# Maximum over the partitions on GpSimd in place of two small matmuls, with four adapter groups computed later

## The reference, cut to what matters

```python
# x (2, 2048, 512), cond (2, 128); norm_w (512, 128), up_w (4096, 512), down_w (512, 2048)
scale = cond @ norm_w.T + 1.0
ms = jnp.mean(x * x, axis=-1, keepdims=True)
h = x * (scale[:, None, :] * jax.lax.rsqrt(ms + EPS))
u = h @ up_w.T
val, gate = jnp.split(u, 2, axis=-1)
h = val * jax.nn.gelu(gate, approximate=False)
x = act_quant(h) @ weight_quant(down_w).T + x
# the second layer: an adapter whose weights depend on cond
Wd_b = Wd + ((cond @ Wdd.T + bdd) * 0.1).reshape(B, BN, D)      # Wdd (65536, 128)
Wu_b = Wu + ((cond @ Wdu.T + bdu) * 0.1).reshape(B, D, BN)
down = jax.nn.relu(jnp.einsum('bld,bnd->bln', x, Wd_b) + bd)
out = x + jnp.einsum('bln,bdn->bld', down, Wu_b) + bu
```

## Time and profile before

| | us |
|---|---|
| median of 3 runs (865.81 to 866.25) | 865.9 |
| the profiled execution | 866.98 |
| its span, first to last instruction | 865.2 |
| TensorE busy | 846.8 (98%) |
| VectorE busy | 608.4 (70%) |
| ScalarE busy | 389.9 (45%) |
| GpSimd busy | 73.9 (9%) |

### The profile page before, as it was taken

How to read it: one execution, slowest core, us unless ns; L and a number is a source line. 1 busy time by engine, 2 the same in 40 slices (tenths; PEclk the granted TensorE clock), 3 DMA queues, 4 the chain that set the end, 5 groups by cost and what they waited for, 6 DMA issues and landing times.

```text
span 865.2 us, 11930 instructions
## 1 busy us (share of the span) xinstructions
PE 846.8 (98%) x4026; PEld 373.9 (43%) x4026; DVE 608.4 (70%) x942; ACT 389.9 (45%) x632; POOL 73.9 (9%) x79
## 2 busy tenths in 40 slices
PE   6999999999999999999999999999999999999998
PEld 5334444444444444444444444444444444444443
DVE  5997666888897765547886664658986764445986
ACT  5678776767545542216545543216433332214000
POOL 0453223210200000000200000000200000000100
PEclk9999999999999999999999999999999999999999
DMA  9879988659788876556587674634447443432231
GB/s 347 308 242 306 332 282 306 219 174 325 246 297 303 312 252 219 204 192 206 207 309 240 230 277 144 203 108 137 144 133 223 137 160 119 159 104 85 98 122 73
DMA packets 64283, 183.50 MB, mean 212 GB/s; under 512 B 7008, under 2 KB 8032, under 8 KB 64224
## 3 DMA queue, kind: packets, MB, share of 16 engines
q1 hardware_dynamic: 63936, 182.48, 60.5%
q10 hardware_dynamic: 288, 0.26, 0.1%
HBM read 152.31 MB, written 29.36 MB: 210 GB/s over the span
## 4 chain that ended last, share of the span: by engine, by line
PE 90%; ACT 3%; DVE 3%; DMA 2%; issue 2%; SPq 0%; POOL 0%; ACTq 0%; DVEq 0%; POOLq 0%
PE aux_ps L1114 10%; PE b_ps L1025 9%; PE b_ps L1029 9%; PE b_ps L1027 9%; PE a_ps L1025 6%; PE a_ps L1027 6%; PE a_ps L1029 6%; PE aux_ps L1070 6%; PE aux_ps L1177 3%; PE aux_ps L1168 3%; PE c_ps L1029 3%; PE c_ps L1027 3%; PE c_ps L1025 3%; PE e_ps L1027 3%; PE e_ps L1029 3%; PE e_ps L1025 3%
## 5 line engine op out<-in xcount | busy, mean ns | idle before, releaser
L1513 DVE SCALAR_TENSOR_TENSOR h_ring<-v_sb,unscale,gelu 128x512 f32<-128x512 f32 x63 | 48.4, 768 | 97.7 <-ACT gelu L836 54.8
L812 ACT ACTIVATE b_ps<-a_ps 128x512 f32<-128x512 f32 x63 | 36.7, 582 | 152.7 <-PE a_ps L1029 152.7
L1025 PE MATMUL b_ps<-t_mov,u_l 128*128 128x512 f16 x252 | 95.5, 379 | 1.6 <-DVE c_ps L1474 1.6
L1029 PE MATMUL b_ps<-t_mov,u_l 128*128 128x512 f16 x252 | 95.5, 379 | 0.0
L1027 PE MATMUL b_ps<-t_mov,u_l 128*128 128x512 f16 x252 | 95.5, 379 | 0.0
L1537 DVE TENSOR_TENSOR hmax<-gelu,hmax 128x512 f32<-128x512 f32 x120 | 82.4, 687 | 6.6 <-ACT gelu L842 1.0
L1114 PE MATMUL aux_ps<-h_ring,wq 128*128 128x512 f16 x384 | 84.9, 379 | 0.3
L711 POOL PARTITION_ALL_REDUCE yscale<-hmax x8 | 17.9, 2266 | 603.0 <-DVE hmax L1537 602.3
L842 ACT ACTIVATE gelu<-h_ring 128x512 f32<-128x512 f32 x64 | 40.3, 630 | 53.0 <-DVE h_ring L1523 52.0
L846 ACT ACTIVATE gelu<-h_ring 128x512 f32<-128x512 f32 x64 | 40.3, 630 | 51.1 <-DVE h_ring L1513 51.1
L1523 DVE SCALAR_TENSOR_TENSOR h_ring<-b_ps,unscale,gelu 128x512 f32<-128x512 f32 x64 | 47.9, 749 | 21.7 <-PE b_ps L1029 21.6
(11 more groups left out here) (217 smaller groups left out, 1640.8 us busy)
## 6 DMA issues: line engine op xcount, KB each, us to landing
w_ring<-in_Wdu SPq DMA_DIRECT2D x64, 512.0 KB, 6.2
w_ring<-in_Wdd SPq DMA_DIRECT2D x56, 512.0 KB, 6.9
u_l<-ul_dram SPq DMA_DIRECT2D x48, 512.0 KB, 4.5
u_e<-ue_dram SPq DMA_DIRECT2D x48, 384.0 KB, 3.1
h_ring<-in_up_w SPq DMA_DIRECT2D x16, 512.0 KB, 7.1
x_sb<-in_x SPq DMA_DIRECT2D x8, 1024.0 KB, 8.1
res<-in_down_w SPq DMA_DIRECT2D x16, 512.0 KB, 6.3
ul_dram<-u_l SPq DMA_DIRECT2D x15, 512.0 KB, 7.6
```

The costliest lines, as they stand in the source:

```text
L1025: pe.matmul(ps[:, :], weight(n, p, 0, k), hi, start=fresh and k == 0, stop=False, skip_group_check=True)
L1029: mm = pe.matmul(ps[:, :], weight(n, p, 1, k), hi, start=False, stop=k == 1, skip_group_check=True)
L1513: dve.scalar_tensor_tensor(out=h_slot(n)[:, TB:TS], in0=val[:, :], scalar=unscale[:, s // 2, j:j + 1], in1=gelu2[:, :], op0=ALU.mult, op1= ...
```

## The change

The maximum over the partitions is taken by GpSimd: `bound(j)` is an all-reduce of column j of `um` into column j of `um_all`, which leaves the maximum in every partition. It stands ahead of `weight_sums(j)`, for j from 1 to 15. DVE clips it and keeps the exponent in place, in `u_scale(j)`, on all partitions. `bounds` of PE, the copies of the power by matmul, and `power(j)` for j over 0 are gone; `first_bounds`, `first_powers` and `first_power` serve chunk 0 as before. `u_scale(j + 1)` of quads 2 to 14 stands at the head of DVE's quad, and `u_low(3, 0)` of quad 2 behind `seed_c(2)`. In quad 1 of ACT `keep_p5(1)` comes ahead of `u_high(2, 0)` and `row_sums(4)`. `DW_QUADS` puts groups 8 to 21 into quads 1 to 15 (14 groups) and groups 22 to 63 into quads 16 to 42. Lines that only rename are left out below.

```diff
-DW_QUADS = ((1, EARLY), (NP, 26), (43, NG))
+DW_QUADS = ((1, EARLY), (NP, 22), (43, NG))
...
     work = [("dw", g) for g in groups_of_quad(n)]
-    if n + 2 < NP:
-        work.append(("bounds", n))
...
-    uses = [("scale", 0), ("stat", 0), ("turn", 0), ("bounds", -2)]
-    uses += [("dw", g) for g in range(4)] + [("bounds", -1)]
-    uses += [("dw", g) for g in range(4, EARLY)]
+    uses = [("scale", 0), ("stat", 0), ("turn", 0)]
+    uses += [("dw", g) for g in range(EARLY)]
...
+        um_all = sb("um_all", [P, NP])
...
+            def bound(j):
+
+                pool.wait_ge(s_um, j + 1)
+                pool.partition_all_reduce(um_all[:, j:j + 1], um[:, j:j + 1], P, AR.absmax)\
+                    .then_inc(s_bound, 1)
+
...
             pool.wait_ge(s_rs, 2)
             for j in SUM_ORDER:
+                if j:
+                    bound(j)
                 weight_sums(j)
...
                 seed_b(n)
-                if n == 1:
-                    u_high(2, 0)
-                    row_sums(4)
...
                 keep_p5(n)
+                if n == 1:
+                    u_high(2, 0)
+                    row_sums(4)
...
-            def bounds(n):
-
-                ps = take("bounds", n)
-                if n + 3 < NP:
-                    pe.wait_ge(s_um, n + 4)
-                    mm = pe.transpose(ps[0:1, 0:P], um[:, n + 3:n + 4], ident[:, :])
-                if n >= -1:
-                    pe.wait_ge(s_top, n + 3)
-                    mm = pe.matmul(ps[:, P:P + 1], ones[0:1, :], um_top[0:1, 0:1], start=True,
-                                   stop=True)
-                mm.then_inc(s_aux, 1)
-
...
-            def u_scale(j, pow_):
-                aux_ready(dve, "bounds", j - 2)
-                u_multiplier(j, pow_)
-                u_unscale(j, pow_)
+            def u_scale(j):
+                top = um_all[:, j:j + 1]
+                bits = top.bitcast(I32)
+                dve.wait_ge(s_bound, j)
+                link(dve.tensor_scalar(top, top, 1e-30, None, ALU.max))
+                link(dve.tensor_scalar(bits, bits, EXP_MASK, None, ALU.bitwise_and))
+                u_multiplier(j, top)
+                u_unscale(j, top)
...
-            power(1)
...
-            u_scale(1, bank("bounds", -1)[:, P:P + 1])
-            power(2)
+            u_scale(1)
...
-            u_scale(2, bank("bounds", 0)[:, P:P + 1])
-            power(3)
+            u_scale(2)
...
                 last = j == NP - 1 and s + 1 < NSB
+                if s == 0 and 1 < j and j + 1 < NP:
+                    u_scale(j + 1)
                 if s == 0 and j > 1:
                     u_low(j, 2)
                     u_low(j, 3)
...
                 if s == 0:
-                    if 1 < j and j + 1 < NP:
-                        u_scale(j + 1, bank("bounds", j - 1)[:, P:P + 1])
-                    if 1 < j and j + 2 < NP:
-                        power(j + 2)
-                    if 1 < j and j + 1 < NP:
+                    if 2 < j and j + 1 < NP:
                         u_low(j + 1, 0)
...
                     seed_c(n)
+                    if n == 2:
+                        u_low(3, 0)
                     multiply1(n - 1)
```

More of the change, by code:

```diff
@@ L377, in build @@
         s_us = sem("s_us")
+        s_bound = sem("s_bound")
         s_first_hi = sem("s_first_hi")
@@ L426, in bank_free @@
                 "turn": (s_top, 1),
-                "bounds": (s_top, i + 4) if i + 3 < NP else (s_umul, 3 * (i + 2) + 3),
                 "mean": (s_mean, 1),
@@ L1198, in _ @@
             stat1(1)
-            bounds(-2)
             stat1(2)
@@ L1210, in _ @@
             adapter_group(3)
-            bounds(-1)
             pe.wait_ge(s_xs, 2 * KD)
@@ L1229, in _ @@
                     product(n, 7)
[L1230 to L1233, removed]
+                for g in groups_of_quad(n):
+                    adapter_group(g)
+                for key in side_work(n)[len(groups_of_quad(n)):]:
+                    if key[0] == "stat":
                         stat(key[1])
@@ L1236, in _ @@
                         spread_rs(key[1])
-                    elif key[0] == "bounds":
-                        bounds(key[1])
                     elif key[0] == "mean":
@@ L1288, in link, with first_power @@
                 dve.wait_ge(s_chain, links[0])
[L1290 to L1297, removed]
+            def first_power():
+                aux_ready(dve, "turn", 0)
+                top, bits = um_top[0:1, 0:3], um_top[0:1, 0:3].bitcast(I32)
+                row = bank("turn", 0)[0:1, 0:P * 3].rearrange("p (n m) -> p n m", n=3)
                 link(dve.tensor_reduce(top, row, AX_X, ALU.max))
@@ L1646, in _ @@
             rsqrt(0)
-            power(0)
+            first_power()
             first_scales()
```

## The result

The changed kernel takes 976.5 us as the median of four runs (972.5 to 976.8), the kernel before 866.1, 110.4 us less. The ratio, taken over all runs, is 1.126, with a 95% interval of 1.123 to 1.129. The forecast of 1008 us was 31.5 us too high and its range of 945 to 1075 holds the result. The profiled execution took 972.48 us for a span of 970.8, 105.6 us more span than before; it is the fastest of the four, and the other three lie at 976.3 to 976.8, so some 4 us of the median stand in no trace.

The account below looks back on a forecast made before the run. PE bounds the kernel before; GpSimd's reload chain was to bound the first superblock. Product 5 of quad 15 138.8 us later plus 3.7 for two pairs: 866.98 + 142.5 - 1.1 is 1008 us, range 945 to 1075.

Parts of the forecast that it names:

- The deciding step: GpSimd, first superblock: each change between all-reduce and tensor_tensor reloads code, 30 times, 8.0 us each (ends 6.2 and 9.9).
- Rival 2: GpSimd reloads much shorter because fetched code lies near: at 4 us each, 888 us; chance 0.05.
- rival 3: GpSimd reloads only at the first call of a kind: 858 us, at best 855; chance 0.04.
- The first reload: GpSimd, ahead of the first all-reduce: charged 8.0 us, after the roots are done at 24.6 us.
- The other 29: GpSimd's remaining reloads before the sums of chunk 15 are done, taken at 8.0 us each.
- rival 1: GpSimd reloads at the quiet end, 6.2 us each: 954 us, or 941 with all-reduces at 0.28; chance 0.15.
- 15 all-reduces: GpSimd's one-column all-reduces, one a chunk for chunks 1 to 15: 1.2 us each, between 0.28 and 2.27.
- The sums: GpSimd's tensor_tensors for 16 chunks: 55.2 us busy, as before, beginning at 24.6 us.
- With both full of PE work this is nought: Two pairs moved to quads 16 to 42: 3.7 us leaves one PE stretch and enters another, net nought.
- the 3.7 charged: PE behind the first superblock: two pairs more at 1.86 us each, lost because the first superblock gets another limit.
- PE's gain: First superblock: small transposes and matmuls gone, 7.7 us less PE work, counting nothing as it lies in idle time.
- Signs: Trace: some 64 MODIFY_POOL_CONFIG, 6 to 10 us issue idle, 18 to 24 us period, some 150 us new PE idle.

Follow-up runs that it names:

- same_code: The kernel after with each bound's all-reduce replaced by a tensor_tensor on the same column, so no maximum for chunks 1 to 15: 873.6 us.
- sums_dve_18: The kernel after with the 64 tensor_tensors of the sums moved to VectorE and 18 groups in the first superblock: 864.1 us.
- reduce_pool_18: The kernel after with 18 groups, the maximum by GpSimd tensor_reduce into one partition, spread by PE's one-column matmul: 864.4 us.
- before_14: The kernel before with 14 groups in the first superblock, nothing else changed: 879.9 us.
- same_code_18: The kernel after with tensor_tensor in place of each bound's all-reduce (no maximum for chunks 1 to 15) and 18 groups in the first superblock: 859.0 us.
- groups_18: The kernel after with 18 groups in the first superblock: 974.3 us.
- before_18_early: The kernel before, 18 groups, with a pair's loads issued one quad earlier wherever the quad before has no pair: 864.2 us.
- no_groups: The kernel after with no adapter group in quads 0 to 15, all 56 later ones in quads 16 to 42: 971.0 us, a single run.
- pairs: The kernel after with two chunks' all-reduces run back to back ahead of both chunks' sums, reloads before the last sums 16 instead of 30: 889.6 us.

## Why the prediction was right, and where it was off

**The deciding step held.** GpSimd going back and forth reloads code each time, 30 times before the last sums, in one chain on one engine. The 64 MODIFY_POOL_CONFIG and same_code show it: with the same order and the same waits, but one kind of operation, 103 us disappear; sums_dve_18 and reduce_pool_18 take the alternation away in two other ways, compute everything, and end 2.9 and 2.6 us under the kernel before. Rival 2 (short reloads) and rival 3 (a reload for the first call only) fall with the rows of the profile.

**The size, term by term**, against the profiled execution. The last sums were to end at 337.8 us and ended at 298.2, 39.6 us sooner:
- The first reload was charged and is hidden: 8.0 us. I put it behind the wait for the roots; its pair of MODIFY_POOL_CONFIG ran at 11.8 us, ahead of that wait.
- The other 29 were charged 8.0 us and took 7.5: 15.0 us. The value lay between the ends given; rival 1 at 6.2 was too low for the mean, though it is just what a reload towards the all-reduce took. That 8.0 came so close is partly luck: it was taken for one price that follows DMA's share, and it is the mean of two kinds, 6.2 and 8.7 us, which the share alone doesn't order (see the last section).
- 15 all-reduces at 1.2 us took 7.0 us, not 18: 11.0 us. The row that it is like in size would have been the better guide.
- The sums took 50.1 us, not 55.2: 5.1 us. A single one takes from 0.72 to 1.7 us in either kernel, and fewer are long now. That DVE's work beside them makes the long ones was not tested. The start at 24.1 gives the last 0.5 us.

Behind that, the product was to start 4.4 us after all four operations of the sums. ACT needs only the first two of them, done at 296.86 us, so the start came 2.0 us after the last one: 2.4 us. Together that is the 42 us between 342.2 and 300.25.

These five all erred to the same side, 42 us together. Some 5 us to the other side behind product 5 (below) and some 5 us by which the profiled execution lies lower against its median than before make that the 31.5 us by which the forecast was too high.

**The step that failed** is "With both full of PE work this is nought", on the 14 groups. A pair costs PE 1.86 us only if its 2 MB are there. The placement decides that: 12.8 to 14.6 us were lost with 14 groups where PE was the bound (before_14 against the kernel before; same_code against same_code_18), of which 2.4 to 3.3 stay with early loads. I looked at DMA's share, 0.80, "with room", and not at which load stands ahead of which in SP's queue. In the kernel after this is mostly covered by GpSimd's chain, which is why the sum could do without it. What is left of it sits behind product 5: the rest of the kernel is 8.7 us longer, not the 3.7 charged. The pair of quad 15 alone takes 4.2 us (308.12 to 312.33) where it took 1.86, and PE has two waits that the kernel before has not, 1.6 us for c_ps and 0.7 us for ACT to empty a bank. That is 4.6 of the 5.0 us.

**PE's gain was there, but no kernel run here that computes the maximum has it whole.** The prediction gave 7.7 us for the small matmuls, and same_code_18, which leaves the maximum out, is 7.5 us under the kernel before. sums_dve_18 takes the same small matmuls from PE and computes the maximum, and gains 2.9 us; reduce_pool_18 keeps the one-column matmul and gains 2.6 us. The change fails on the choice of the operation, not on the engine: in reduce_pool_18 GpSimd takes the maximum without a loss.

**Signs.** The period came to 18.7 us a chunk (33.39 to 295.35 over 14 chunks), within the 18 to 24 given. The reloads took 5.8 to 11.9 us, not 6 to 10; five of the 29 are above 10. The new idle time on PE is 80.5 us, not 150: partly because the whole was smaller, partly because PE's matmuls took longer at the lower clock, 25 us more busy time in all with less work. The first all-reduce ran at 24.1, not 34.5. The clock was not charged, and whether it cost anything on the path was not tested.

The Trainium skill, GPSIMD Engine Reference, section 2.1 (Instruction dispatch), gives about 6 us (5.95) for the load ahead of a first call. The runs agree for most reloads towards the all-reduce, 5.6 to 6.7 us, and not as one figure for all: towards tensor_tensor they took 6.7 to 11.9 us in the kernel after and without groups, and up to 12.7 us in groups_18.

## What to carry to other kernels

Before putting a second kind of operation on GpSimd, look for MODIFY_POOL_CONFIG at the edges of the kinds that are there, and ask whether the new one shares its code with its neighbours; if not, count two reloads of 6 to 12 us, as here, for each time it is used, or choose an operation that does share it, or move one of the two. A change that moves loads in one engine's busy queue is not neutral because PE's work is: read what stands ahead of them, and issue them a step early where the buffers allow. Take a change of several parts apart, since the larger loss can hide the smaller one: here some 14 us stood behind 103. And compare an edit with the kernel that has the same edit and nothing else: against the kernel before, the early loads seemed to take away the whole loss of the 14 groups; against before_18_early they leave 2.4 us.

## What the runs showed of the hardware

How long a reload takes differs with its direction and with the loads that SP has just issued. The windows are the reloads themselves, in the kernel after; the columns are stretch, its length, busy time and instructions of PE, PEld, DVE, ACT and POOL, then clock, DMA share and GB/s. The first four end with a tensor_tensor, the last three with an all-reduce:

```profile
118.40:128.80 10.40, 8.39 (x43) 2.88 (x41) 5.12 (x12) 2.09 (x4) 0.00 (x0) 1.00 1.00 359
...
158.90:169.20 10.30, 9.24 (x45) 3.15 (x43) 4.49 (x12) 1.36 (x3) 0.03 (x1) 0.99 0.99 341
...
252.40:259.60 7.20, 7.20 (x29) 3.01 (x28) 6.41 (x14) 2.26 (x4) 0.03 (x1) 0.84 0.19 76
...
287.80:295.30 7.50, 4.87 (x24) 2.04 (x23) 6.93 (x15) 1.08 (x2) 0.00 (x0) 1.00 0.17 70
...
77.20:85.80 8.60, 6.76 (x24) 2.51 (x22) 0.03 (x1) 0.60 (x1) 0.02 (x1) 0.80 0.96 303
...
131.70:137.50 5.80, 2.80 (x8) 1.07 (x9) 3.25 (x5) 5.80 (x12) 0.03 (x1) 0.80 0.05 8
...
172.00:178.00 6.00, 2.93 (x10) 1.20 (x11) 2.65 (x4) 6.00 (x13) 0.10 (x1) 0.85 0.10 24
```

The DMA share alone doesn't order them. Towards tensor_tensor a reload took 7.2 to 7.5 us at a share below 0.2 and 10.3 to 10.5 us at 1.0, but also 7.0 us at shares of 0.82 and 0.86 (up to 222.85 and 93.25 us) and 11.9 us at 0.68 (up to 149.84). What the five over 9.5 us have in common is their start: each begins 0.6 to 1.3 us after SP has begun to issue the four 512 KB loads of a pair or a 1 MB load of x, and no shorter one towards tensor_tensor does. Towards the all-reduce it is 5.8 to 6.6 us, at shares up to 0.43, with one exception, the 8.6 us at 77.2; that one starts with a 1 MB load of x, and it takes 8.3 and 8.0 us in groups_18 and no_groups, where no pair's loads follow the x, and 11.1 us in pairs, where they do. This is what goes together in the traces, and no_groups is the only run that takes loads away to see.

And the pair of MODIFY_POOL_CONFIG runs ahead of a wait that stands before the operation in the program (at 11.8 us, where the wait for the roots ended at 24.1), so that this reload cost no time of its own.
